# A Mamba-2 block with a LoRA feed-forward gate: x and B turned to token rows by DVE 32x32 transposes and a DRAM round trip, x scaled on ACT and POOL

## The reference

```python
x = L0_attn_hidden_states
xn = _layernorm(x, axis=-1)
s = _L0_attn_ref(xn, ...)
g = _silu(_L0_ffn_ref(xn, ...))
x = x + s * g
```

```python
proj = einsum('bld,pd->blp', hidden_states, in_proj_w)   # gate | x, B, C | dt
conv = conv_bias + sum of 4 shifted products with conv_weight
xBC = silu(conv);  x, Bm, Cm = split(xBC)
dt_p = softplus(dt + dt_bias);  dA = exp(dt_p * -exp(A_log));  dtx = dt_p[..., None] * x
def step(state, inp):
    state = state * dA_t[..., None, None] + dtx_t[..., None] * B_t[:, :, None, :]
    y_t = einsum('bhpn,bhn->bhp', state, C_t)
y = ys + x * D;  yn = y * rsqrt(mean(y*y over a group) + EPS) * norm_weight * silu(gate)
out = einsum('bli,di->bld', yn, out_proj_w)
```

## Time and profile before

| what | value |
|---|---|
| median of 3 runs | 1794.66 us (1794.21 to 1797.45) |
| profiled execution, first to last instruction | 1793.2 us |
| PE busy | 1759.6 us, 98% |
| DVE busy | 1522.7 us, 85% |
| POOL busy | 1145.6 us, 64% |
| ACT busy | 836.0 us, 47% |
| mean granted TensorE clock | 0.998 |

### The profile page before, as it was taken

The page is one execution under the profiler, slowest core; times in us unless marked ns, Lnnn a source line. Parts: engine busy times, 40 slices in busy tenths (PEclk is TensorE's granted clock), DMA queues, the critical chain, the costliest instruction groups (busy, mean ns, idle before and its releaser), DMA issues.

```text
span 1793.2 us, 30683 instructions
## 1 busy us (share of the span) xinstructions
PE 1759.6 (98%) x11416; PEld 1417.5 (79%) x11416; DVE 1522.7 (85%) x1936; ACT 836.0 (47%) x1923; POOL 1145.6 (64%) x1143
## 2 busy tenths in 40 slices
PE   8999999999999999999999999999999999999997
PEld 5778878888887888888777788888888888888875
DVE  7868888888888888888888988889898888989887
ACT  4554453544435354443534434354444535444465
POOL 6537566565756656575697847648574664757567
PEclk9999999999999999999999999999999999999999
DMA  8533333232332323333574333323233332324234
GB/s 267 159 124 113 123 98 133 100 108 105 106 130 87 137 107 106 106 107 124 172 233 143 120 110 127 109 95 123 90 119 117 114 122 94 119 94 129 95 112 147
DMA packets 113508, 220.78 MB, mean 123 GB/s; under 512 B 10448, under 2 KB 46672, under 8 KB 113360
## 3 DMA queue, kind: packets, MB, share of 16 engines
q1 hardware_dynamic: 112320, 218.66, 36.2%
q10 hardware_dynamic: 1040, 0.16, 0.0%
HBM read 204.63 MB, written 14.16 MB: 122 GB/s over the span
## 4 chain that ended last, share of the span: by engine, by line
PE 83%; DVE 8%; ACT 4%; issue 2%; POOL 2%; DMA 1%; SPq 0%; ACTq 0%; DVEq 0%; POOLq 0%
PE ps_conv L1304 9%; PE ps_conv L1307 9%; PE ps_y L1478 6%; PE ps_conv L1310 6%; PE ps_out L1304 6%; PE ps_out L1307 6%; PE ps_gate L1304 6%; PE ps_gate L1307 6%; PE ps_y L1483 5%; PE ps_s L1515 5%; PE ps_out L1310 4%; PE ps_gate L1310 4%; PE turned_x L1395 3%; DVE xc L885 2%; PE ps_conv L1311 2%
## 5 line engine op out<-in xcount | busy, mean ns | idle before, releaser
L885 DVE SCALAR_TENSOR_TENSOR xc<-ps_conv,convw_sb,xc 128x511 f32<-128x511 f32 (+2 forms) x576 | 430.3, 747 | 153.9 <-ACT xc L651 140.3
L1237 POOL TENSOR_TENSOR rstd_col<-mean_square,half 128x1 f32<-128x1 f32 x128 | 89.4, 698 | 533.2 <-ACT mean_square L794 533.2
L1009 DVE TENSOR_TENSOR_SCAN decay<-decay,eye 128x1024 f32<-128x1024 f32 x125 | 294.7, 2358 | 0.9 <-DMA decay<-decays_d 0.9
L657 ACT ACTIVATE xc<-xc 128x512 f32<-128x512 f32 x192 | 121.0, 632 | 322.0 <-DVE xc L885 320.6
L1226 POOL TENSOR_TENSOR cpre<-cpre,xc 128x1024 f32<-128x1024 f32 x112 | 268.8, 2400 | 0.0
L1304 PE MATMUL ps_conv<-xn_hi,wconv_hi 128*128 128x512 f32 x768 | 242.0, 437 | 0.0
L1307 PE MATMUL ps_conv<-xn_hi,wconv_lo 128*128 128x512 f32 x768 | 207.4, 392 | 0.0
L1478 PE MATMUL ps_y<-decay,dtx 128*64 128x128 f32 x1984 | 190.9, 279 | 3.6 <-DVE decay L1030 2.8
L1304 PEld LDWEIGHTS ps_conv<-xn_hi,wconv_hi 128*128 128x128 f32 x768 | 141.4, 194 | 49.3 <-issue 27.2
L803 ACT ACTIVATE square<-ps_y 128x512 f32<-128x512 f32 x126 | 75.6, 600 | 220.8 <-DVE ps_y L1062 220.8
L1483 PE MATMUL ps_y<-cpre,state 128*64 128x128 f32 x1760 | 171.3, 273 | 0.0
(11 more groups left out here) (241 smaller groups left out, 3860.4 us busy)
## 6 DMA issues: line engine op xcount, KB each, us to landing
decay<-decays_d SPq DMA_DIRECT2D x125, 512.0 KB, 5.4
cpre<-rows_d SPq DMA_DIRECT2D x112, 512.0 KB, 3.9
stage<-w_in_t SPq DMA_DIRECT2D x32, 1024.0 KB, 6.6
stage<-w_out_t SPq DMA_DIRECT2D x16, 1024.0 KB, 5.5
stage<-w_in_t SPq DMA_DIRECT2D x32, 256.0 KB, 3.1
out_sum<-hidden SPq DMA_DIRECT2D x16, 256.0 KB, 5.6
ffn_d<-sgate SPq DMA_DIRECT2D x16, 256.0 KB, 2.8
out<-out_sum SPq DMA_DIRECT2D x16, 256.0 KB, 3.6
```

Of the source, the lines that this page charges most:

```text
L885: e.scalar_tensor_tensor(acc[:, d:], ps[:, 0:BLK - d], convw_sb[:, tile, TAPS - 1 - d:TAPS - d], acc[:, d:], ALU.mult, ALU.add).then_inc(S ...
L1009: e.tensor_tensor_scan(d, d, eye8[:, :, :].rearrange("p h i -> p (h i)"), 0.0, ALU.mult, ALU.add).then_inc(scanned(i)[0], 1)
```

## The change

x and B of a chunk no longer go through PE. On DVE one transpose instruction turns the 32x32 blocks of the five tiles (four of x, one of B) of step `i + 1` into `squares`. SP stores them with four DMAs into `turned_d` in DRAM and loads them back with two (`x_tok`, `b_tok`, two buffers each), now in token rows. ACT multiplies with the step sizes in every step (`dtx`, eight operations of 64 columns), and `mean_square` moves ahead of the silu on ACT. POOL multiplies x with the last factors (`scale_x`). The diff, cut to its core:

```diff
+            def store_turned(i):
+                w.wait_ge(S["turned"], i + 1)
+                w.wait_ge(landed_tok[i % 2], 32 * (i // 2))
+                for a in range(QUADS):
+                    e.dma_start(turned_d[i % 2, :, a, :].rearrange("(b j) c -> j b c", j=SQ),
+                                squares[a * SQ:(a + 1) * SQ, :, :, :].rearrange("j b t i -> j b (t i)")
+                                ).then_inc(S["st_turned"], 16)
+            def fetch_tokens(i):
+                w.wait_ge(S["st_turned"], 16 * QUADS * (i + 1))
...
+                e.dma_start(x_tok[i % 2][:, :, :, :].rearrange("p a t i -> p a (t i)"),
+                            turned_d[i % 2, :, :, 0:P]).then_inc(landed_tok[i % 2], 16)
+                e.dma_start(b_tok[i % 2][:, :].rearrange("p (a i) -> p a i", i=SQ),
+                            turned_d[i % 2, :, :, P:P + SQ]).then_inc(landed_tok[i % 2], 16)
...
 (SP, in a step)
                 if i + 1 < N and (i + 1) % NCH:
                     fetch_rows(i + 1)
+                if i + 1 < N:
+                    store_turned(i + 1)
...
+                if i + 1 < N:
+                    fetch_tokens(i + 1)
...
 (ACT, in a step)
                     conv(conv_late(i))
+                if u >= 0:
+                    w.wait_ge(S["mm_ssq"], u + 1)
...
+                    e.activation(mean_square[:, u % 2:u % 2 + 1], ps_g[:, 2 * P:2 * P + 1], ACT.Identity, bias=eps[:, :],
+                                 scale=1.0 / GC).then_inc(S["var2"], 1)
                 if 0 <= m < N and conv_late(m) is not None:
                     silu(conv_late(m))
...
+                if i < N:
+                    w.wait_ge(landed_tok[i % 2], 32 * (i // 2 + 1))
...
+                    for h in range(GH):
+                        scaled = e.activation(dtx[i % 2][:, h * HD:(h + 1) * HD].rearrange("p (a i) -> p a i", i=SQ),
+                                              head_of(x_tok[i % 2], h), ACT.Copy, scale=steps[:, first + h:first + h + 1])
+                    scaled.then_inc(S["dtx"], 1)
-                if i < N and at < NCH - 1:
-                    w.wait_ge(S["mm_bt"], inner(i))
-                    e.activation(b_tok[:, :], ps_g[:, 0:P], ACT.Copy).then_inc(S["b_tok"], 1)
...
 (DVE)
+            def turn(i):
+                nb = i // CPB
+                w.wait_ge(S["silu"], max(conv_no(nb, t) for t in range(TT)) + 1)
+                w.wait_ge(S["st_turned"], 16 * QUADS * i)
+                e.transpose(squares[:, :, :, :].rearrange("p b t i -> p t b i"),
+                            xc[nb % 2][:, 0:TT, block_cols(i % NCH)].rearrange("p t (b j) -> p t b j", j=SQ)
+                            ).then_inc(S["turned"], 1)
...
-                    if i < SCALED_DTX:
-                        e.tensor_tensor(by_head(dx[:, :]), by_head(turned_x[:, :]), heads_bc(step_size), ...
                     if i <= TAIL:
                         scan(i)
-                    if c < NCH - 1 and i < SCALED_XW:
-                        e.tensor_tensor(by_head(xw[:, :]), by_head(turned_x[:, :]), ...
+                    if i + 1 < N:
+                        turn(i + 1)
...
 (POOL, behind rstd_col and the splits, ahead of cpre)
+            def scale_x(i):
+                w.wait_ge(landed_tok[i % 2], 32 * (i // 2 + 1))
+                w.wait_ge(*lasts(i))
...
+                e.tensor_tensor(xw[:, :].rearrange("p (t a i) -> p t a i", t=XT, a=QUADS), x_of(x_tok[i % 2]),
+                                weight.unsqueeze(3).to_broadcast([P, XT, QUADS, SQ]), ALU.mult).then_inc(S["xw"], 1)
...
 (PE)
-            def turn_xc(i):
-                for t in range(XT):
-                    tr = e.transpose(turned_x[:, t * P:(t + 1) * P], xc[nb % 2][:, t, block_cols(i % NCH)], eye)
...
-                    e.transpose(ps_g[:, 0:P], xb[:, XT, cc], eye).then_inc(S["mm_bt"], 1)
...
-                    w.wait_ge(S["pt"], 3 if i < 3 else 4)
-                    w.wait_ge(S["b_tok"], inner(i))
+                    w.wait_ge(S["pt"], len(RATES))
+                    w.wait_ge(landed_tok[i % 2], 32 * (i // 2 + 1))
                     w.wait_ge(S["xw"], inner(i))
...
-                    e.matmul(ps_s[:, :], b_tok[:, :], xw[:, :], start=True, stop=True).then_inc(S["mm_u"], 1)
+                    e.matmul(ps_s[:, :], b_tok[i % 2][:, :], xw[:, :], start=True, stop=True).then_inc(S["mm_u"], 1)
```

More of the change, by code:

```diff
@@ L20 @@
 MT = XT + 2
+TT = XT + 1
+QUADS = P // SQ
 BLK = 512
@@ L90, in tile_order @@
 def tile_order(nb):
-    return (1, 0, 3, 2, 5, 4) if nb == NB // 2 else tuple(range(MT))
+    return (1, 0, 3, 2, 4, 5) if nb == NB // 2 else tuple(range(MT))
 def conv_no(nb, m):
@@ L191, in build @@
         xw = sb("xw", [P, GC])
-        b_tok = sb("b_tok", [P, NS])
+        squares = sb("squares", [P, QUADS, TT, SQ])
+        x_tok = [sb(f"x_tok{i}", [P, QUADS, XT, SQ]) for i in range(2)]
+        b_tok = [sb(f"b_tok{i}", [P, NS]) for i in range(2)]
         square = sb("square", [P, GC])
@@ L208, in build @@
         edge_in = sb("edge_in", [P, MT, TAPS - 1])
-        last = [sb(f"last{i}", [P, GH, 1]) for i in range(3)]
+        last = [sb(f"last{i}", [P, GH, 2]) for i in range(3)]
         ones = sb("ones", [P, 1])
@@ L241, in build @@
             landed_rows0 landed_rows1 st_rows10 st_rows11 st_rows00 st_rows01
-            mm_t dtx scan last xw mm_bt b_tok mm_g M skip cpre mm_gate sgate mm_in mm_u
+            turned st_turned landed_tok0 landed_tok1 dtx scan last xw mm_g M skip cpre mm_gate sgate mm_in mm_u
             y state sdec square sum1 sum2 mm_ssq var2 rstd2 yg hi2 lo2 mm_out osum
@@ L333, in chunk_cols, with head_of, x_of @@
             return slice(c * P, (c + 1) * P)
+        def head_of(tokens, h):
+            return tokens[:, h % 2 * 2:h % 2 * 2 + 2, h // 2, :]
+        def x_of(tokens):
+            return tokens[:, :, :, :].rearrange("p a t i -> p t a i")
         def block_cols(c):
@@ L773, in _ @@
                     split_hi(wout_hi, staged(0, DM), range(XT), S["hi_out"])
-                if SCALED_DTX <= i < N:
-                    w.wait_ge(S["mm_t"], i + 1)
-                    w.wait_ge(landed_prefix[at], 32)
+                if i < N:
+                    w.wait_ge(landed_tok[i % 2], 32 * (i // 2 + 1))
+                    if batch(i) == 0:
+                        w.wait_ge(S["pt"], 3 + at // CPB)
+                    else:
+                        w.wait_ge(landed_prefix[at], 32)
                     w.wait_ge(S["mm_in"], i - 1)
                     first = at * P + HEADS + g % GROUPS * GH
-                    for h in range(GH - 1):
-                        e.activation(dtx[i % 2][:, h * HD:(h + 1) * HD], turned_x[:, h * HD:(h + 1) * HD], ACT.Copy,
-                                     scale=steps[:, first + h:first + h + 1])
-                    e.activation(dtx[i % 2][:, (GH - 1) * HD:], turned_x[:, (GH - 1) * HD:], ACT.Copy,
-                                 scale=steps[:, first + GH - 1:first + GH]).then_inc(S["dtx"], 1)
-                if i < N and at < NCH - 1:
-                    w.wait_ge(S["mm_bt"], inner(i))
-                    w.wait_ge(S["mm_u"], inner(i) - 1)
-                    e.activation(b_tok[:, :], ps_g[:, 0:P], ACT.Copy).then_inc(S["b_tok"], 1)
-                if u >= 0:
-                    w.wait_ge(S["mm_ssq"], u + 1)
-                    w.wait_ge(S["rstd2"], u - 1)
-                    w.wait_ge(S["half"], 2)
-                    if i < N and at < NCH - 1:
-                        w.wait_ge(S["mm_bt"], inner(i))
-                    e.activation(mean_square[:, u % 2:u % 2 + 1], ps_g[:, 2 * P:2 * P + 1], ACT.Identity, bias=eps[:, :],
-                                 scale=1.0 / GC).then_inc(S["var2"], 1)
+                    for h in range(GH):
+                        scaled = e.activation(dtx[i % 2][:, h * HD:(h + 1) * HD].rearrange("p (a i) -> p a i", i=SQ),
+                                              head_of(x_tok[i % 2], h), ACT.Copy, scale=steps[:, first + h:first + h + 1])
+                    scaled.then_inc(S["dtx"], 1)
                 if 0 <= m < N:
@@ L803, in _ @@
                     e.activation(square[:, :], y_bank(m)[:, :], ACT.Square).then_inc(S["square"], 1)
-                if SCALED_XW <= i < N - 1:
-                    w.wait_ge(S["mm_t"], i + 1)
-                    w.wait_ge(*lasts(i))
-                    w.wait_ge(S["mm_u"], inner(i) - 1)
-                    for h in range(GH - 1):
-                        e.activation(xw[:, h * HD:(h + 1) * HD], turned_x[:, h * HD:(h + 1) * HD], ACT.Copy,
-                                     scale=last_room(i)[:, h, 0:1])
-                    e.activation(xw[:, (GH - 1) * HD:], turned_x[:, (GH - 1) * HD:], ACT.Copy,
-                                 scale=last_room(i)[:, GH - 1, 0:1]).then_inc(S["xw"], 1)
                 if i < N and conv_early(i) is not None:
@@ L970, in _ @@
                         rate(q, part_of(q, n))
+                if s == GATE_AT + 3:
+                    turn(0)
             def fin(f, sums):
```

(5 more changed lines are left out.)

51 lines of the change are left out of this document (20 added, 31 removed).

## The result

| | before | after |
|---|---|---|
| median of the runs | 1794.43 us (4 runs, 1793.64 to 1797.45) | 1867.4 us (4 runs, 1866.54 to 1867.85) |
| profiled span | 1793.2 us | 1866.0 us |

The ratio is 1.040, its 95% interval 1.0387 to 1.0415: slower by 73 us where I forecast 28. The direction held, and four of the six terms of the sum came within 5 us, two of them in part by luck. The term that decides, chunk 1, I had put at half of what it is.

The account below looks back on a forecast made before the run. It took PE, busy 98% of the span, as the bound: 1793.2 - 65 + 36 + 29 + 15 + 11 + 3 = 1822 us of span, so 1823 for the median of the runs. Its own range was 1805 to 1850, the wider one 1785 to 1890.

Parts of the forecast that it names:

- chunk 1: PE's wait before mm_u for xw, behind POOL's four splits: 2.25 us, 16 times, 36 us.
- PE sheds: Transposes of x and B leave PE, which bounds the kernel: 65 us less, 85 by the other end.
- chunk 3: PE's wait before mm_u for xw, behind POOL's splits: 1.9 us, 15 times, 29 us.
- chunks 4 and 5: POOL's backlog makes xw late for PE: 0.3 to 0.8 us in chunk 4, about the same in 5; 15 us.
- chunk 7: ACT's dtx delays the square and gating, so PE's product waits for the mixing matrix: 0.75 us, 15 times, 11 us.
- first tokens: Nothing covers the DRAM round trip for step 0: about 3 us.
- What POOL gets: xw, 1.04 us on POOL, stands behind the splits and mm_u waits for it; the term that decides.
- Rival 2: POOL or DVE lose more to each other; DVE's transpose delays splits 0.8 us in 61 steps: 49 us, 1872; chance 0.10.
- Rival 1: PE's clock falls in the new waits of 1.9 and 2.25 us: up to 53 us more, 1876; chance 0.15.
- The round trip: Tokens stored to DRAM and loaded back stay hidden in a median landing, except for step 0, about 3 us.

Follow-up runs that it names:

- number 8: The kernel before the change, with each of the four transposes of x done twice on PE: 1840.5 us, ratio 1.025 to the kernel before.
- Numbers 3: The changed kernel with DVE's scan in chunk 1 cut to 128 of 1024 columns: 1834.2 us, ratio 1.022 to the kernel before.
- 11: The changed kernel with ACT's mean_square behind the silu again: 1860.6 us, ratio 1.036 to the kernel before.
- number 1: The changed kernel with POOL making xw ahead of the splits: 1797.6 us, ratio 1.0015 to the kernel before.
- Number 7: The changed kernel with xw before the splits, wconv_lo's splits in chunk 2, dtx behind y's square, step 1's tokens stored and fetched early: 1876.4 us, ratio 1.045.
- number 4: The changed kernel with xw made on DVE, ahead of the turn, in place of POOL: 1816.1 us, ratio 1.0125 to the kernel before.

## Why the prediction was wrong in size

By its own terms. The measured ones come from the lengths of all steps of a chunk, summed, before and after (chunk 1: 222.6 and 288.0 us; 3: 197.0 and 222.7; 4: 188.8 and 186.2; 5: 230.8 and 230.8; 7: 171.1 and 173.6), each difference with 0.50 us a step added for what PE sheds (the same sums of chunk 2: 237.0 and 227.0, of 6: 228.9 and 221.0). In chunk 1 the wait is how much later PE comes to `mm_u` than T + 5.74 (at 8.99 by the median), and the slow clock what the rest of the step takes over 8.5 us (10.13).

| term | forecast, us | measured, us |
|---|---|---|
| PE sheds | -65 | 128 x 0.50 = -64 |
| chunk 1 | 36 | 73: wait 15 x 3.25 = 49, slow clock 13 x 1.63 = 21, 3 in two steps with waits of 4.5 and 4.8 |
| chunk 3 | 29 | 34 |
| chunks 4 and 5 | 15 | 13 |
| chunk 7 | 11 | 10 |
| first tokens | 3 | 7, of which 3.6 are `xw` behind the splits of step 1 |
| sum | 29 | 73 |

**What PE sheds: right.** Chunks 0, 2 and 6 show it at 0.50 to 0.56, number 8 the part of x at 0.40 to 0.44 the other way round.

**What POOL gets: the step that failed.** I wrote "POOL splits from 1.75 to 6.8". Each duration in it was right (`xw` 1.05 against 1.04, four splits 4.99 against 5.04), but not that of the first operation, `rstd_col`, which I took from a step where nothing ran beside it: it took 2.29 us for 0.59, since it ended with DVE's scan. The row to see it by was before me: the state took 3.03 us beside a scan. The kernel before even shows it on `rstd_col` itself, in step 43 (T at 678.73), where it took 0.84 us and ended 0.35 behind the scan. So does every `rstd_col` of over 0.8 us, 33 in that trace and 44 in the changed kernel's:

```profile
677.94 2.28 DVE L1009 TENSOR_TENSOR_SCAN decay<-decay,eye 128x1024 f32<-128x1024 f32 x1
...
679.73 0.84 POOL L1237 TENSOR_TENSOR rstd_col<-mean_square,half 128x1 f32<-128x1 f32 x1 [8.08 <-ACT mean_square L794]
```

`mean_square` is 2 us earlier in chunk 1 than before, where it stood behind four high halves, and so `rstd_col` falls into the scan. Rival 2 had this very mechanism and gave it to the transpose, where it isn't: beside the turn (672.14 to 672.98) four splits took 4.99 us. Numbers 3 and 11 show it is the scan.

**Rival 1 came true in chunk 1.** The longer wait brought the slow clock, at 1.63 us each. I gave it 0.15 since most of my waits were shorter than that of the earlier trace rows; by my own numbers they weren't, 16 of the 31 were 2.25 us against 2.08. In chunk 3 (1.98 us) the clock stayed up in all 15 steps. With the right wait and this rival in chunk 1 alone the sum would have been 1822 + 13 + 21 = 1856.

**Chunk 3: right**, within 5 us. Its splits began at T + 1.73 and not 1.4, since here too `rstd_col` (1.15 us) ended with the scan.

**Chunks 4 and 5: right within 2 us, in part by luck.** `rstd_col` started 1.61 us after T in chunk 4 by the median, where I had 1.7 to 2.2. But by the medians the two chunks lost 0.13 and 0.37 us, half of the 1.0 a group that I had; 7 of the 13 us are from there, and 6 from four steps alone (60, 61, 124 and 125).

**Chunk 7: size by luck, cause half right.** The 15 steps I had meant lost 0.43 us each, not 0.75; that is 6.5 us, and 3.9 come from step 127, which I had put at zero. The mechanism I gave is in the trace: `dtx` ends at T + 2.97 (I had 3.0), and the gating waits 0.37 us for the square behind it. What I left out is that `mean_square` ahead of the silu also holds DVE's turn (0.33 us). With the silu first (number 11) 0.27 of the 0.43 go although the gating still waits for `dtx`; the 0.16 that stay no run here takes apart.

**The round trip: right, but for both ends.** In the last three steps ACT waited 3.5 us for tokens. PE's wait in step 1 was 7.5 us, where I had spoken of step 0 alone: with `xw` ahead of the splits the first T comes 3.6 us earlier (number 1), and 3.8 us stay. DVE had turned its squares by 115.14, but their store stands on SP behind the rows, the totals and the decays and is issued at 120.15; the fetch, which waits for it to land, comes at 128.95:

```profile
120.15 2.75 SPq L483 DMA_DIRECT2D turned_d<-squares  x4
128.95 0.56 SPq L494 DMA_DIRECT2D x_tok<-turned_d  x1
...
134.98 2.04 PE L1537 MATMUL ps_s<-xw,b_tok 128*128 128x512 f32 x2 [7.48 <-POOL xw L1266]
```

I had asked for what is queued behind the waiting SP and not for what the new stores queue behind. Number 7 shows that the order there is a choice between two waits.

**The rules of the Trainium skill.** `xw` took 1.05 us on POOL and 0.69 on DVE (number 4), 1.5 times. The Trainium skill, "GPSIMD Engine Reference", section "Performance versus the Vector engine", has 1.96 times, measured on an add of 2048 columns; by it I would have added 18 us that aren't there. `rstd_col` took 0.55 us alone and 2.29 beside the scan, four splits beside the turn no longer than without it. The Trainium skill, "SBUF — State Buffer", section "SBUF: two separate sides", says that a VectorE operation with two inputs in SBUF and a GpSimd operation that reads SBUF shut each other out for the whole instruction, whichever starts first. The scan has two inputs in SBUF and the turn one, so the trace agrees.
